# The transposes of the q and k stacks: SyncE's DMAs in place of TensorE and VectorE

## What is computed

```python
# x: (32, 256, 128), 16 heads of 8
def reference(x, ...):
    xn = _layernorm(x)
    x = x + _L0_attn_ref(xn, ...) + _L0_ffn_ref(xn, ...)
    xn = _layernorm(x)
    return x + _L1_attn_ref(xn, ...) + _L1_ffn_ref(xn, ...)

def _L0_attn_ref(x, Wq, Wk, Wv, Wo, bo):
    Q = _l2norm(heads(Wq)); K = _l2norm(heads(Wk)); V = heads(Wv)
    cos_sim = jnp.clip(jnp.einsum('bhtd,bhsd->bhts', Q, K), -0.999, 0.999)
    W = jnp.power(jnp.maximum(1.0 - jnp.arccos(cos_sim) / jnp.pi, EPS), 16.0)
    W = W / (jnp.sum(W, axis=-1, keepdims=True) + EPS)
    return jnp.einsum('bhts,bhsd->bhtd', W, V) ... @ Wo + bo

def _L0_ffn_ref(x, W_qkv, b_qkv, W_gate, b_gate, W_experts, b_experts):
    # softmax attention of 16 heads, plus the two best of 8 experts per token
    return attn_out + moe_out
```

## Time and profile before

| what | us |
|---|---|
| median of 3 runs | 1978.48 |
| lowest and highest of the runs | 1976.43, 1978.59 |
| the profiled execution | 1968.91 |
| its span, first to last instruction | 1967.1 |
| ACT busy, in the span | 1778.4 |
| DVE busy | 1761.1 |
| PE busy | 1475.6 |
| POOL busy | 1183.2 |
| DVE's copies to stkT (L871), 128 of them | 84.6 |
| PE's transposes of stk (L1056), 1024 of them | 81.8 |

### The profile page before, as it was taken

One profiled execution on the slowest core, in us unless ns is written; L12 is line 12 of the kernel. 1 busy time (PEld: TensorE's weight loads), 2 busy tenths in 40 slices (PEclk: granted clock), 3 DMA queues, 4 the chain that ended last, 5 costly groups with the idle time before them and its releaser, 6 DMA issues.

```text
span 1967.1 us, 38505 instructions
## 1 busy us (share of the span) xinstructions
PE 1475.6 (75%) x12022; PEld 751.1 (38%) x12022; DVE 1761.1 (90%) x3977; ACT 1778.4 (90%) x1888; POOL 1183.2 (60%) x540
## 2 busy tenths in 40 slices
PE   2677778777778777777878777778778778777765
PEld 1223434333443433344343334434334434333333
DVE  5779998999999999999999999999999999999864
ACT  1299999999999999999999999999999999999993
POOL 1556666666666666666666656665666666665640
PEclk9667898889888988988898888898888888888876
DMA  1000000000000000000000000000000000000000
GB/s 42 3 4 1 6 1 6 5 6 6 6 5 0 6 5 6 6 6 5 0 6 5 6 6 6 0 6 6 5 6 5 6 0 6 6 5 6 4 3 6
DMA packets 21058, 11.19 MB, mean 6 GB/s; under 512 B 1431, under 2 KB 20953, under 8 KB 20956
## 3 DMA queue, kind: packets, MB, share of 16 engines
q1 hardware_dynamic: 20956, 10.20, 1.8%
HBM read 6.00 MB, written 4.19 MB: 5 GB/s over the span
## 4 chain that ended last, share of the span: by engine, by line
DVE 37%; issue 22%; ACT 20%; PE 18%; DVEq 2%; SPq 0%; POOL 0%; ACTq 0%; DMA 0%; POOLq 0%
ACT curve L578 10%; DVE nmax L885 6%; DVE curve L875 5%; ACT root L578 4%; PE psM L1045 4%; DVE curve L879 3%; PE psM L1037 3%; DVE acc L859 3%; DVE xn L781 1%; PE psS L1095 1%; DVE h L454 1%; PE psM L1207 1%; PE psM L1190 1%; DVE stkT L871 1%; ACT prob L578 1%
## 5 line engine op out<-in xcount | busy, mean ns | idle before, releaser
L530 POOL TENSOR_TENSOR root<-curve 128x2048 f32<-128x2048 f32 x128 | 478.9, 3741 | 453.2 <-DVE curve L879 453.2
L578 ACT ACTIVATE curve<-curve 128x2048 f32<-128x2048 f32 x384 | 719.1, 1907 | 5.6 <-POOL curve L533 2.2
L578 ACT ACTIVATE root<-root 128x2048 f32<-128x2048 f32 x256 | 484.7, 1906 | 0.0
L533 POOL TENSOR_TENSOR curve<-curve,root 128x2048 f32<-128x2048 f32 x64 | 354.6, 5562 | 65.2 <-ACT root L578 65.2
L879 DVE TENSOR_SCALAR curve<-psS 128x1024 f32<-128x1024 f32 x256 | 308.2, 1215 | 2.7 <-PE psS L1068 1.9
L885 DVE TENSOR_REDUCE nmax<-psS 128x4 f32<-128x1024 f32 x256 | 302.7, 1213 | 0.9 <-PE psS L1077 0.9
L578 ACT ACTIVATE prob<-psS 128x1024 f32<-128x1024 f32 x256 | 256.6, 1029 | 32.8 <-PE psS L1097 31.1
L566 POOL TENSOR_TENSOR stk<-qk,stk 128x512 f16<-128x512 f32 x128 | 148.1, 1167 | 73.4 <-ACT stk L578 72.9
L1045 PE MATMUL psM<-we,xnT 128*128 128x512 f32 x256 | 172.4, 762 | 0.0
L875 DVE TENSOR_TENSOR curve<-curve,root 128x2048 f32<-128x2048 f32 x64 | 161.0, 2516 | 6.1 <-ACT root L578 6.1
L1077 PE MATMUL psS<-stkT 32*128 32x256 f16 x1024 | 103.1, 294 | 80.7 <-DVE curve L879 42.5
(11 more groups left out here) (194 smaller groups left out, 2818.0 us busy)
## 6 DMA issues: line engine op xcount, KB each, us to landing
xt<-in_L_attn_x SPq DMA_DIRECT2D x32, 128.0 KB, 2.2
out<-yo SPq DMA_DIRECT2D x32, 128.0 KB, 1.8
we<-in_L_ffn_W_experts SPq DMA_DIRECT2D x1, 512.0 KB
curve<-in_L_attn_w_qkv SPq DMA_DIRECT2D x1, 192.0 KB
curve<-in_L_ffn_w_down SPq DMA_DIRECT2D x1, 176.0 KB
curve<-in_L_ffn_w_gate SPq DMA_DIRECT2D x2, 64.0 KB
curve<-in_L_ffn_w_up SPq DMA_DIRECT2D x2, 64.0 KB
curve<-in_L_ffn_W_qkv SPq DMA_DIRECT2D x1, 128.0 KB
```

What stands on the lines that cost most here:

```text
L530: nc.gpsimd.tensor_tensor(root[:, two], curve[:, p, two], curve[:, p, two], ALU.mult).then_inc(s_sq, 1)
L533: nc.gpsimd.tensor_tensor(curve[:, p, two], curve[:, p, two], root[:, two], ALU.mult).then_inc(s_half[0], 1)
L578: return nc.scalar.activation(out, in_, func, **kw)
```

## The change

SP issues the transposes. Its list gets four stages `stackT` between the load and the store; each waits for the stack of its kind (`s_stk`) and for the batch before to be done with `stkT`, and then issues two transposing DMAs, one per token half, from 128 x 512 of `stk` to 128 x 4 x 128 of `stkT`. Each kind has a semaphore on which its DMAs land. The stages `stackT` leave PE's and DVE's lists and the PSUM ring. The readers c and m wait for the landings of their two kinds; POOL's and ACT's writers of the high parts wait for the landing of the batch before, in place of PE's transposes. The half-precision identity is dropped.

```diff
 ORDER = {
     "sync": [
-        ("load", 0, 1), ("down", 0, -2),
+        ("load", 0, 1), ("stackT", 0, 1), ("stackT", 1, 1), ("stackT", 2, 1), ("stackT", 3, 1), ("down", 0, -2),
     ],
     "tensor": [
...
-        ("stackT", 0, 1), ("stackT", 1, 1), ("pvf", 2, 0), ("m", 0, 1), ("m", 1, 1), ("p1", 0, -1), ("m", 2, 1),
-        ("stackT", 2, 1), ("pvf", 3, 0), ("stackT", 3, 1), ("m", 3, 1), ("xqT", 0, -1), ("m", 4, 1), ("hT", 0, -2),
-        ("hT", 1, -2), ("c", 0, 1), ("gu", 0, -1), ("m", 5, 1), ("m", 6, 1), ("gu", 1, -1), ("c", 1, 1), ("m", 7, 1),
-        ("down", 0, -2),
+        ("pvf", 2, 0), ("m", 0, 1), ("m", 1, 1), ("p1", 0, -1), ("m", 2, 1), ("pvf", 3, 0), ("m", 3, 1),
+        ("xqT", 0, -1), ("m", 4, 1), ("hT", 0, -2), ("hT", 1, -2), ("c", 0, 1), ("gu", 0, -1), ("m", 5, 1),
+        ("m", 6, 1), ("gu", 1, -1), ("c", 1, 1), ("m", 7, 1), ("down", 0, -2),
...
-        s_stkTp, s_stkT = sem("stackT_in_psum", 4), sem("stackT_ready", 4)
+        s_stkI = sem("stackT_begun", 4)
+        s_stkT = [sem(f"stackT_{name}_landed", 32) for name in ("cosine_q", "cosine_k", "softmax_q", "softmax_k")]
...
+                if stage == "stackT":
+                    kind = KINDS[arg]
+                    sp.wait_ge(s_stk, due(s_stk, b, arg + 1))
+                    if kind < 2:
+                        sp.wait_ge(s_c, due(s_c, b - 1))
+                    else:
+                        sp.wait_ge(s_m, due(s_m, b - 1))
+                        sp.wait_ge(s_e, due(s_e, b - 1))
+                    sp.sem_inc(s_stkI, 1)
+                    for j in range(NT):
+                        sp.dma_start_transpose(
+                            stkT[:, kind, :, j * P:(j + 1) * P],
+                            stk[:, kind, j * HEADS:(j + 1) * HEADS, :, :].rearrange("p h s d -> p (h s d)")).then_inc(s_stkT[kind], 16)
...
-                    pool.wait_ge(s_stkTp, due(s_stkTp, b - 1, arg + 1))
+                    pool.wait_ge(s_stkT[kind], due(s_stkT[kind], b - 1))
...
-                    act.wait_ge(s_stkTp, due(s_stkTp, b - 1, arg + 1))
+                    act.wait_ge(s_stkT[kind], due(s_stkT[kind], b - 1))
...
-                if stage == "stackT":
-                    kind = KINDS[arg]
-                    bank, k = misc_bank(stage, arg, 0)
-                    dve.wait_ge(s_stkTp, due(s_stkTp, b, arg + 1))
-                    if kind < 2:
-                        dve.wait_ge(s_c, due(s_c, b - 1))
-                    else:
-                        dve.wait_ge(s_m, due(s_m, b - 1))
-                        dve.wait_ge(s_e, due(s_e, b - 1))
-                    nc.vector.tensor_copy(stkT[:, kind, :, :], bank16[k]).then_inc(s_stkT, 1)
...
-                if stage == "stackT":
-                    kind = KINDS[arg]
-                    bank, k = misc_bank(stage, arg, 0)
-                    last, value = bank_read(stage, arg, 0, t)
-                    pe.wait_ge(last, value)
-                    pe.wait_ge(s_stk, due(s_stk, b, arg + 1))
-                    cols = stk[:, kind, :, :, :].rearrange("p (j g h) s d -> p j g (h s d)", j=NT, g=4)
-                    for g in range(4):
-                        for j in range(NT):
-                            ins = transpose(bank16[k][:, g, j * P:(j + 1) * P], cols[:, j, g, :], ident16[:, :])
-                    ins.then_inc(s_stkTp, 1)
...
-                    pe.wait_ge(s_stkT, due(s_stkT, b))
+                    for kind in (0, 1):
+                        pe.wait_ge(s_stkT[kind], due(s_stkT[kind], b))
...
-                    pe.wait_ge(s_stkT, due(s_stkT, b, 2))
+                    for kind in (2, 3):
+                        pe.wait_ge(s_stkT[kind], due(s_stkT[kind], b))
```

More of the change, by code:

```diff
@@ L75 @@
         ("choose", 0, 1), ("xn1T", 0, -1), ("quantx", 0, -1), ("newton", 0, 1), ("quantx", 1, -1), ("quantx", 2, -1),
[L76 to L80, removed]
+        ("choose", 1, 1), ("quantx", 3, -1), ("quantx", 4, -1), ("quantx", 5, -1), ("quantx", 6, -1),
+        ("choose", 2, 1), ("quantx", 7, -1), ("m", 0, 1), ("m", 1, 1), ("quantx", 8, -1), ("p1", 0, -1),
+        ("choose", 3, 1), ("m", 2, 1), ("m", 3, 1), ("m", 4, 1), ("mul", 1, 0), ("c", 0, 1), ("hmul", 0, -1),
+        ("m", 5, 1), ("m", 6, 1), ("mul", 3, 0), ("hmul", 1, -1), ("choose", 4, 1), ("quanth", 0, -1), ("c", 1, 1),
         ("m", 7, 1), ("down", 0, -2),
@@ L103 @@
 USES = {"xnT": 1, "proj": 2, "maxT": 1, "finc": 1, "ocT": 1, "wo": 1, "xn1T": 1, "p1": 2, "s1": 1, "p1T": 1, "o1": 1,
-        "xqT": 1, "gu": 2, "finf": 1, "stackT": 1, "experts": 2, "hT": 1, "down": 1}
+        "xqT": 1, "gu": 2, "finf": 1, "experts": 2, "hT": 1, "down": 1}
 MISC = [(s, a, use) for s, a, lag in ORDER["tensor"] for use in range(USES.get(s, 0))]
@@ L155, in build @@
         ident = sb("ident", [P, P])
-        ident16 = sb("ident16", [P, P], F16)
         identb = sb("identb", [P, P], BF16)
@@ L264, in build @@
         psM = [psum(f"psM{k}", [P, 512]) for k in range(2)]
-        bank16 = [p[:, :].bitcast(F16).rearrange("p (g t) -> p g t", g=4) for p in psM]
         bankb = [p[:, :].bitcast(BF16).rearrange("p (g t) -> p g t", g=4) for p in psM]
@@ L371, in build @@
             READ[("hT", j, 0)] = (s_hT, j + 1)
-        for kind in range(4):
-            READ[("stackT", kind, 0)] = (s_stkT, kind + 1)
         def bank_read(stage, arg, use, t, uses=MISC):
@@ L519, in _ @@
                         link(nc.gpsimd.memset(v[:, k, j, :, 0:3:2, HD:HD + 1], 1.0))
-            nc.gpsimd.tensor_copy(ident16[:, :], ident[:, :])
             nc.gpsimd.tensor_copy(identb[:, :], ident[:, :]).then_inc(s_const, 1)
```

## The result

| what | before | after |
|---|---|---|
| median of the runs, us | 1978.0 | 2086.55 |
| lowest and highest | 1976.43, 1978.59 | 2076.98, 2102.78 |
| the profiled execution, us | 1968.91 | 2076.98 |
| ACT's waits, 330 to 1765 us, sum a step | 2.1 | 5.7 |
| granted clock in that stretch | 0.87 | 0.81 |

The change makes the kernel slower: the ratio is 1.0571 (1.0539 to 1.0603), 108 us, or 3.4 us in each of 32 steps. The medians here are of the runs made beside one another, four of each.

A forecast was written before the change was run, and what follows sets the result against it. ACT's work plus its waits around the projections was taken as the bound; 1.9 (past the budget) + 0.5 (clock) - 0.35 (gain) = 2.1 us a step, 67 us in 32, gave 2045 us, range 1964 to 2200.

The forecast's parts named there:

- ACT sets the period: The step is ACT's work plus two waits around the projections; time freed on DVE mostly becomes longer waiting at L802.
- rival (c): DVE was the bound after all: its 2.4 us a step come back, 1902 us; chance below 1 in 50.
- The budget of 4.3 us: On PE, m 0 may start up to 4.3 us after the last e ends before ACT waits at u1T.
- gap: Time from the end of the last e to m 0, while four DMAs are issued and land: 6.2 us.
- The pitch: Time between successive transposing DMAs on SP: 1.1 us, from pieces of 256 bytes, midway between overlapped and non-overlapped issue.
- The landing: Time from a transposing DMA's issue to its arrival: a plain load's 2.2 us plus 0.43 us of pieces, 2.63.
- Rival (a): Transposing DMAs have a plain copy's pitch and landing, nothing is late: 1967 us, or 1978 with low clock; chance 0.30.
- Rival (b): Transposing DMAs are slow, 5.2 or 6.9 us each, so c 0 is late too: about 3000 or 3480 us; chance 0.16.
- The clock: PE idles before m 0, so p1 and its neighbours run at the low granted clock: 0.5 us a step added.
- The gain of 0.35 us: ACT's waits at mT, xqT and lnv, behind DVE's copies, go: 0.35 us a step, 11 us in 32.
- Kinds 0 and 1 in time: Their DMAs land near 916.7, before c 0 at 917.04, which itself moves by two us; no cost counted.
- DVE's busy time: Dropping four copies a step on DVE lowers its busy time by about 85 us.

The follow-up runs named there:

- dbl: The changed kernel with a second stkT buffer for kinds 2 and 3, so their DMAs start when the stacks are ready: 1978.81 us, ratio 1.0031.
- wide: The changed kernel with one 1024-column DMA a kind instead of two of 512, stkT's token half ahead of the group: 1986.93 us, ratio 1.005.
- widewarm: wide with 12 dummy products ahead of m 0 on PE and choose 3 ahead of m 0 on DVE: 1980.95 us, ratio 1.0025.
- shapes: The changed kernel with the same bytes in DMAs of 512, 256, 512 and 128 columns by stage, 16 issues a step instead of 8: 2326.11 us.
- cos_dma: The kernel before with only kinds 0 and 1 (cosine q and k) transposed by SP's DMAs: 1989.79 us, ratio 1.0098.
- late_choose: The kernel before with choose 3 one place later in DVE's order, behind m 2: 2081.08 and 2091.32 us in the two runs compared.
- dblwarm2: dbl with 14 dummy products ahead of m 0 and 8 ahead of m 3 on PE, choose 3 ahead of m 0 on DVE: 1982.11 us, ratio 1.0031.

## Why the prediction was right, and where its terms were off

**ACT sets the period: right.** The 2.4 us a step that DVE gets back shorten nothing, even in `dbl`, where ACT doesn't wait at u1T; rival (c) had 77 us for it and is out. (`dbl`'s lower clock hides some of a gain, but its price at p1T is 8.2 us in 25 steps.)

**The budget of 4.3 us: right.** A wait at u1T of gap - 4.3 + (m 0 to u1T) - 1.25 closes in three kernels: the changed one 6.82 - 4.3 + 0.67 = 3.19 against 3.22 measured, `wide` 4.97 - 4.3 + 0.68 = 1.35 against 1.39, `widewarm` 5.01 - 4.3 - 0.06 = 0.65 against 0.62 (e ended there at 858.67).

**The pitch: the term mis-sized, and its reason wrong.** I took 1.1 us, from pieces of 256 bytes; it is 1.34. The pieces exist: (160220 - 20956) / 256 = 544 packets a DMA, 512 of 256 bytes and 32 more. But they don't set the pitch. At 512 columns SP's issue does, 1.26 of the 1.34 us, and `shapes` has 1.12 to 1.31 us for DMAs with as little as a quarter of the pieces. The working had 0.46 us for an issue, so that 1.1 came out this near to 1.34 is luck. At 1024 columns the issue is still 1.24 us but the pitch 1.79, and what makes up the rest is open. The landing came out at 2.5 for 2.63. So the gap is 6.82 and not 6.2 us, 0.6 a step.

Rival (a) was nearly right on the landing, 2.5 us against the 2.2 of the earlier trace rows, and wrong on the issue, 1.26 against 0.40. The rule behind it, that transposing DMAs are as fast as regular ones, is that of the Trainium skill, "Advanced Engine Details and Errata", section X-Bar Transpose (TRN2); in this trace it holds for the landing and not for the issue. Rival (b) falls: four blocks in one DMA cost one issue and 2.5 us to land. The Trainium skill, "VectorE: DVE Perf Modes", section The three transpose paths, has 1309 ns for a block; here the blocks of a DMA don't go one after another at that price.

**The clock: 0.67 us for 0.5.** `widewarm` against `wide` shows this part by itself, as far as the wait at u1T goes. The clock has another price that I left out: behind 15 us at 0.50 to 0.51 ACT waits 2.4 to 2.8 us at p1T, from 330 to 1765 us in two steps of the changed kernel and in three each of `cos_dma` and `dbl`. In the kernel before, that clock is 0.82 or more in every step of the stretch, and ACT never waits there.

**The gain of 0.35 us: wrong.** The wait at mT went as I had said, from 5.9 to 0.7 us. But h, xqT and p1T took its place, with 18.8 us against 4.4 (4.9 of it are the two waits at p1T; for h and xqT no run shows the cause), and the waits other than u1T grew by 0.4 us a step. With the measured terms the step loses 2.52 + 0.67 + 0.4 = 3.6 us, 115 in 32, where I had 2.1 and 67; 108 were measured.

**Kinds 0 and 1 in time: right.** The last DMA is issued at 894.33 + 7 x 1.34 and lands 2.5 us later, at 906.2, ahead of c 0 at 908.36. `shapes` shows the wait that comes past this point. I counted these two kinds at nothing all the same, and `cos_dma` loses 17 us by them. Close to half of what ACT's waits grew by there is the low clock ahead of p1T; the rest isn't explained.

**DVE's busy time: down 62 us, not 85.** The copies, back to back, held the engine 0.60 us each, 77 us in 128; and DVE's product of `curve` by `root` grew from 161.0 to 175.1 us, 2736 ns in the mean instead of 2516. A longer wait for POOL's product, by the lock above, would explain that, but no run tests it.

## What to carry to other kernels

Moving work to an idle engine frees nothing where the busy one isn't the bound: find which wait ends last, then work out how late the moved step may come and what stands behind it in the in-order queues. Count transposing DMAs by issues first and by bytes second: the same transposes in half as many issues cost 11 us instead of 108, though pitch and landing grew at 1024 columns, and with a second buffer, in as many issues, 6. Here TensorE had less to do and a lower granted clock, 0.81 for 0.87: look at the clock of the stages behind the work that was taken away. Before an entry in an order written out by hand is moved, look for a long GpSimd instruction beside its new place.

## What the hardware showed that I had not expected

- A transposing DMA from SBUF to SBUF holds SP for 1.1 to 2.1 us, 1.23 to 1.26 in the median of each kernel, at anything from 128 to 1024 columns of 128 partitions in half precision; a plain copy holds it for 0.4.
- Its landing took 2.4 us in the run of mixed widths, 2.5 at 512 columns and 3.2 at 1024.
- A VectorE instruction of 0.16 us on 128x16 elements took 3.98 to 4.51 us when GpSimd's product on 128x2048 had begun first, and in the wrong place that cost 5.3 and 5.8% of the whole kernel in the two runs of `late_choose` that are compared.
- In the step shown, the clock fell from 1.00 to 0.50 while PE stood idle from 895.17 to 900.99, and PE then worked at 0.50 for 6 us without a pause.
- Where, from 330 to 1765 us, the clock was 0.50 or 0.51 in the 15 us ahead of p1T, ACT waited 2.4 to 2.8 us there, in `cos_dma`, `dbl` and the changed kernel alike; at 0.73 it was 1.46 us, in three steps of `dblwarm2` and `widewarm`.
